# First keys read in halves, the first maxima's rows sent ahead, and unused products in TensorE's wait

## The reference

```python
q, k, v = split(x @ W_qkv.T + b_qkv)                   # 32 x 256 tokens, 16 heads of 8
p = softmax(einsum('bthd,bshd->bhts', q, k) / sqrt(8))
x = layernorm(x + (p @ v) @ W_out.T + b_out)
scores = sigmoid(x @ gate_w.T)                          # 8 experts, the best two of scores + bias
y = shared(x) + sum of two experts(x * score) * score   # each silu(x w1) * (x w3) @ w2
x = layernorm(x + y)
```

## Time and profile before

| | |
|---|---|
| median of the runs | 765.87 us (764.38 to 766.14) |
| the profiled execution | 764.94 us |
| its span, first to last instruction | 763.1 us |
| TensorE busy | 740.5 us, 97% |
| VectorE busy | 630.9 us, 83% |
| ScalarE busy | 521.4 us, 68% |
| GpSimd busy | 500.8 us, 66% |
| mean granted TensorE clock | 0.98 of full speed |

### The profile page before, as it was taken

The page is one execution under the profiler, slowest core; times in us unless marked ns, Lnnn a source line. Parts: engine busy times, 40 slices in busy tenths (PEclk is TensorE's granted clock), DMA queues, the critical chain, the costliest instruction groups (busy, mean ns, idle before and its releaser), DMA issues.

```text
span 763.1 us, 20494 instructions
## 1 busy us (share of the span) xinstructions
PE 740.5 (97%) x7004; PEld 531.6 (70%) x7004; DVE 630.9 (83%) x1353; ACT 521.4 (68%) x1069; POOL 500.8 (66%) x714
## 2 busy tenths in 40 slices
PE   4899999999999999999999999999999999999996
PEld 2456665665666566566554788888888888888886
DVE  6889999999999999999997657988666766666676
ACT  3289899998988889898888646454454544455442
POOL 7356888878777787877624755566565655655564
PEclk8599999999999999999999999999999999999999
DMA  6667666675665556656611745454554544455440
GB/s 171 179 160 190 182 174 185 169 191 162 168 172 156 172 148 169 171 160 174 154 32 43 203 116 115 118 130 117 152 128 128 126 127 129 129 125 124 125 106 29
DMA packets 202369, 108.93 MB, mean 143 GB/s; under 512 B 10537, under 2 KB 202281, under 8 KB 202281
## 3 DMA queue, kind: packets, MB, share of 16 engines
q1 hardware_dynamic: 198560, 105.22, 52.9%
q10 hardware_dynamic: 3720, 2.57, 1.4%
HBM read 73.41 MB, written 33.82 MB: 141 GB/s over the span
## 4 chain that ended last, share of the span: by engine, by line
PE 93%; DVE 2%; DMA 1%; issue 1%; ACT 1%; POOL 1%; ACTq 0%; POOLq 0%; SPq 0%; DVEq 0%
PE bank L1037 17%; PE bank L841 16%; PE bank L810 11%; PE bank L848 9%; PE bank L849 9%; PE bank L850 9%; PE bank L826 8%; PE bank L934 3%; PE bank L904 3%; PE bank L958 2%; PE bank L965 1%; PE bank L990 1%; DVE negmax L1188 1%; PE bank L869 1%; PE bank L974 1%
## 5 line engine op out<-in xcount | busy, mean ns | idle before, releaser
L1188 DVE TENSOR_REDUCE negmax<-bank 128x2 f32<-128x512 f32 x512 | 322.9, 679 | 16.1 <-PE bank L826 13.7
L666 ACT ACTIVATE probs<-bank 128x512 f32<-128x512 f32 x512 | 294.2, 613 | 47.7 <-PE bank L810 43.8
L784 ACT ACTIVATE q_stack<-k_stack 128x512 f32<-128x512 f32 x128 | 80.8, 631 | 152.3 <-DVE k_stack L1247 152.1
L826 PE MATMUL bank<-k_stack,q_stack 48*128 48x256 bf16 x1024 | 163.5, 281 | 8.8 <-DMA q_stack<-q_parts_dram 6.1
L810 PE MATMUL bank<-q_stack,k_stack 50*128 50x256 bf16 x1024 | 157.7, 274 | 0.7 <-ACT probs L666 0.4
L1247 DVE TENSOR_TENSOR k_stack<-bank,probs 128x512 f32<-128x512 f32 x128 | 88.3, 689 | 71.0 <-PE bank L850 69.5
L841 PE MATMUL bank<-probs,v_aug 128*32 128x256 f32 x2048 | 137.6, 386 | 0.2 <-ACT attT L677 0.2
L848 PE MATMUL bank<-x_hi,hi_w 128*128 128x512 f32 x288 | 126.5, 439 | 1.3 <-DVE res L1200 0.5
L810 PEld LDWEIGHTS bank<-q_stack,k_stack 50*128 50x128 bf16 x1024 | 75.9, 95 | 72.2 <-issue 35.3
L849 PE MATMUL bank<-x_hi,lo_w 128*128 128x512 f32 x288 | 114.2, 396 | 0.0
L850 PE MATMUL bank<-x_lo,hi_w 128*128 128x512 f32 x288 | 113.7, 395 | 0.0
(11 more groups left out here) (132 smaller groups left out, 1198.2 us busy)
## 6 DMA issues: line engine op xcount, KB each, us to landing
probs<-route_dram SPq DMA_DIRECT2D x128, 256.0 KB, 5.0
k_stack<-k_parts_dram SPq DMA_DIRECT2D x64, 192.0 KB, 4.1
q_stack<-q_parts_dram SPq DMA_DIRECT2D x62, 192.0 KB, 3.4
q_parts_dram<-q_parts SPq DMA_DIRECT2D x32, 192.0 KB, 2.1
k_parts_dram<-k_parts SPq DMA_DIRECT2D x32, 192.0 KB, 2.2
k_parts_dram<-k_parts SPq DMA_DIRECT2D x32, 128.0 KB, 2.0
q_parts_dram<-q_parts SPq DMA_DIRECT2D x32, 128.0 KB, 2.1
x_sb<-x SPq DMA_DIRECT2D x32, 128.0 KB, 2.2
```

The lines of the kernel that those rows point to most:

```text
L666: nc.scalar.activation(probs[h][:], score_ps[bank(b, h)][:].rearrange("p (j t) -> p j t", j=NT), ACT.Exp).then_inc(exp_done, 1)
L784: nc.scalar.activation(act[n % DEPTH], gated[n % DEPTH] if n else up1_ps[0][:], ACT.Silu).then_inc(act_set, 1)
L826: mm = pe.matmul(max_ps[bank(b, h)][:, i * T:(i + 1) * T], q_stack[b.ring][first:last, h // 2, i * P:(i + 1) * P], k_stack[b.ring][first:l ...
L1188: nc.vector.tensor_reduce(negmax[b.ring % 2][:, :, column], max_ps[bank(b, head)][:].rearrange("p (i s) -> p i s", i=NT), AX_X, ALU.max, n ...
```

## The change

The first batch's keys are read with four DMAs in two halves with a semaphore each. Batch 0's rows of maxima are sent at the head of SyncE's slot -1, and only the first of their two DMAs is SyncE's; the second is ScalarE's, at the end of its slot -1. For batch 0 the transposes move from p = 4 to p = 5, and VectorE's copy from step 9 to step 11. TensorE gets products of a constant tile that nobody reads: four in slot -4, sixteen in slot -2 at p = 3, and one at the head of each pair of slots -2 and -1 in which row maxima are found (four and eight). The constants of the fourth ring are GpSimd's now.

```diff
+            def row_maxima_in(b):                                    # SyncE
+                sp.wait_ge(max_rows_set, b.count(1, 1))
+                for u in range(2 if b.c else 1):
+                    sp.dma_start(q_stack[b.ring][HALF * u + ROWS:HALF * u + ROWS + 2, :, :],
+                                 max_rows[H * u:H * u + H, :]).then_inc(max_in[b.ring], 16)
             def first_stack(b):
                 sp.wait_ge(first_k_out, 16 * PARTS)
-                for u in range(2):
-                    sp.dma_start(k_stack[b.ring][HALF * u:HALF * u + ROWS, :, :],
-                                 k_parts_dram[b.ring].rearrange("(g u) d c t -> u (d c) g t", u=2)[u]).then_inc(first_k_in, 16)
+                for n in range(2):
+                    pairs = slice(n * PAIRS // 2, (n + 1) * PAIRS // 2)
+                    for u in range(2):
+                        sp.dma_start(k_stack[b.ring][HALF * u:HALF * u + ROWS, pairs, :],
+                                     k_parts_dram[b.ring].rearrange("(g u) d c t -> u (d c) g t", u=2)[u][:, pairs, :]).then_inc(first_k_in[n], 16)
             def slot(t):
+                if t.neg.c == 0:
+                    row_maxima_in(t.neg)
                 b = t.stack
...
-                    sp.wait_ge(k_ones, b.c + 1)
+                    if b.c < RING - 1:
+                        sp.wait_ge(k_ones, b.c + 1)
+                    else:
+                        sp.wait_ge(fourth_set, 1)
...
-                b = t.neg
-                if b.live:
-                    sp.wait_ge(max_rows_set, b.count(1, 1))
-                    for u in range(2):
-                        sp.dma_start(q_stack[b.ring][HALF * u + ROWS:HALF * u + ROWS + 2, :, :],
-                                     max_rows[H * u:H * u + H, :]).then_inc(max_in[b.ring], 16)
+                if t.neg.live and t.neg.c:
+                    row_maxima_in(t.neg)
...
+            r = RING - 1                                             # GpSimd
+            pool.memset(k_stack[r][:].rearrange("p h t -> p (h t)").bitcast(F32), TWO_ONES).then_inc(fourth_set, 1)
+            pool.memset(v_aug[r][:], 0.0).then_inc(fourth_set, 1)
+            pool.wait_ge(fourth_set, 2)
+            for u in range(2):
+                ins = pool.memset(v_aug[r][:, :, u, :, 2 * D + u:2 * D + u + 1], 1.0)
+            ins.then_inc(fourth_set, 1)
...
                 if t.proj.live and h == ACT_LOAD:                    # ScalarE, end of its slot
...
+                if t.neg.c == 0:
+                    act_e.wait_ge(max_rows_set, 1)
+                    act_e.dma_start(q_stack[0][HALF + ROWS:HALF + ROWS + 2, :, :], max_rows[H:2 * H, :]).then_inc(max_in[0], 16)
...
-                    pe.wait_ge(first_k_in, 32)                       # TensorE
+                    pe.wait_ge(first_k_in[h // (H // 2)], 32)
...
+            def fill(ps, count):
+                for _ in range(count):
+                    pe.matmul(ps[:], filler[:, 0:P], filler[:], start=True, stop=True)
             def slot(t, first=0, last=PAIRS):
                 for p in range(first, last):
+                    if (t.soft.c, p) == (-4, 0):
+                        pe.wait_ge(filler_set, 1)
+                        fill(max_ps[0], 4)
+                    if (t.soft.c, p) == (-2, PE_VQ + 1):
+                        fill(max_ps[0], 16)
+                        pe.wait_ge(qk_f, 3)
+                    if t.soft.c in (-2, -1) and t.maxima(2 * p)[0].live:
+                        fill(score_ps[0], 1)
...
-                    if b.live and p == PE_TOK:
+                    if b.live and p == (PE_TOK if b.c else PE_TOK + 1):
...
+            dve.memset(filler[:].bitcast(F32), TWO_ONES).then_inc(filler_set, 1)   # VectorE, first
             clear_keys(0)
             clear_keys(1)
             clear_values(0)
...
             clear_values(1)
-            for r in (2, 3):
-                clear_keys(r)
-                clear_values(r)
-            dve.wait_ge(v_clear, 2 * RING)
+            clear_keys(2)
+            clear_values(2)
+            dve.wait_ge(v_clear, 2 * (RING - 1))
...
-                        if t.neg.live:
+                        if t.neg.live and t.neg.c:
                             dve.wait_ge(max_T, t.neg.count(1, 1))
...
-                    if b.live and h == DVE_TOK:
+                    if b.live and h == (DVE_TOK if b.c else DVE_TOK + 2):
+                        if b.c == 0:
+                            dve.wait_ge(max_T, 1)
```

More of the change, by code:

```diff
@@ L116, in attention_moe_layer @@
         attT = sb("attT", [P, 2, T])
+        filler = sb("filler", [P, 512], BF16)
         recip_sum = sb("recip_sum", [P, 8 * NT, 2])
@@ L133, in attention_moe_layer @@
         max_rows_ps = misc[0:2 * H, 3 * P:4 * P].bitcast(BF16)
+        filler_set = sem("filler_set")
         wv_in, bv_in = sem("wv_in"), sem("bv_in")
@@ L140, in attention_moe_layer @@
         wqk_hi_set, wqk_lo_set, xT_hi_set, xT_lo_set = (sem(n) for n in ("wqk_hi_set", "wqk_lo_set", "xT_hi_set", "xT_lo_set"))
+        fourth_set = sem("fourth_set")
         k_ones, v_clear, consts_set = sem("k_ones"), sem("v_clear"), sem("consts_set")
@@ L146, in attention_moe_layer @@
         stack_in = [sem(f"stack_in{r}") for r in range(RING)]
-        first_k_out, first_q_out, first_k_in = sem("first_k_out"), sem("first_q_out"), sem("first_k_in")
+        first_k_out, first_q_out = sem("first_k_out"), sem("first_q_out")
+        first_k_in = [sem(f"first_k_in{n}") for n in range(2)]
         first_q_in = [sem(f"first_q_in{n}") for n in range(2)]
@@ L702, in slot @@
                             act_e.wait_ge(av_mm, b.count(4, 4 * (1 - RING)))
+                        elif b.c < RING - 1:
+                            act_e.wait_ge(v_clear, 2 * (b.c + 1))
                         else:
-                            act_e.wait_ge(v_clear, 2 * (b.c + 1))
+                            act_e.wait_ge(fourth_set, 3)
                         for u in range(2):
```

## The result

The changed kernel takes 770.20 us (median, 768.28 to 770.98) against 765.87: ratio 1.0058, 95% interval 1.0046 to 1.0069. It is 4.3 us slower, outside the range I gave (763.0 to 769.6), and on the side of my slower rival. Its profiled execution has a span of 768.5 us against 763.1, 5.4 us more.

A forecast was written before the change was run, and what follows sets the result against it. TensorE has no pause from about 32 us, so only slot 1's start counts: slot 0 2.3 us later, less 0.6 of half clock, is +1.7 on 764.94, 766.6; the median shown is 0.9 above, 767.6, range 763.0 to 769.6.

The forecast's parts named there:

- my slower rival: Thin work from 15 to 29 us doesn't hold the clock; slot 0 at 37.9, total 771.0; chance 0.14.
- The chain copy, first row DMA, load, ScalarE, second row DMA: Before slot 0: ScalarE's row DMA waits for batch 4's load behind SyncE's; slot 0 starts at 34.6, 2.3 us later.
- clock 1.00 at 13 to 29: A sign to look for: TensorE at full clock from the first wait through the row maxima.
- the clock holds here: In the wait for the queries, sixteen unread products leave 2.4 us idle, under the 3.8 after which the clock fell.
- are hidden: In the row maxima, twelve singles of 0.22 us each at 2.4 GHz fit inside a pair's 1.21 us of reductions.
- At full clock the first reduction starts: Batch 0's maxima: first reduction 0.43 us behind the first product instead of 0.69, at 15.5.
- VectorE's two gaps: In batch 0's maxima, the gaps of 0.59 and 1.45 us shrink to some 0.2 together (0 to 0.8).
- my third rival: The half-clock case in the maxima: slot 0 at 37.9, +5.1 us, total 771.0; chance 0.14.
- The second row DMA: ScalarE's row DMA before slot 0, issued at 31.6 beside batch 2's stack reads, lands in 3.0 us.
- Slot 0: First part at 1.2 GHz, 6.5 us of half clock (5 to 8) against 8.0 before: 0.6 less.
- Clock held to slot 0's end: Rival: clock holds through the wait at 29 to 34.6, slot 0 takes some 10.3; total 765.1; chance 0.32.
- Rows as early as before: Rival: batch 0's rows aren't held by the load, slot 0 starts at 30.6 at full clock; total 761.1; chance 0.12.

The follow-up runs named there:

- e1: The changed kernel with SyncE issuing batch 4's load of x transposed ahead of its wait for the copied maxima; 765.26 us, ratio 0.9999.
- e6: The changed kernel with batch 4's load ahead of the wait for the copied maxima and without the twelve single unread products; 764.15 us, ratio 0.9987.
- e7: The changed kernel with batch 4's load ahead of the wait for the copied maxima, without the sixteen and the twelve unread products; 764.39 us, ratio 0.9989.
- e12: The changed kernel without the twelve single unread products, nothing else; 768.63 us, ratio 1.0048.
- e9: The changed kernel with batch 3's and 4's loads early, three unread products for each single and nine more at slot 0's head; 763.65 us, ratio 0.9983.
- e11: The kernel of e9 with the copy and its transposes back at step 9 and p = 4; 761.70 us, ratio 0.9956.
- e2: The changed kernel with both row DMAs on SyncE, at the same place; 766.44 us, ratio 1.0015.
- e4: The kernel before with all the unread products (4, 16, 12) and nothing else; 765.85 us, ratio 1.0010.
- e5: The changed kernel with batch 4's load ahead of the wait for the copied maxima and batch 3's load at the start; 764.90 us, ratio 0.9995.
- e8: Keys halved, row DMAs split but SyncE's behind stack reads, batch 3's load at start, copy at step 9, only the first four unread products; 764.87 us, 0.9994.
- e3: The kernel before with the keys read in halves and nothing else; 765.12 us, ratio 0.9997.

## Why the prediction was wrong

**Right in mechanism.** The chain copy, first row DMA, load, ScalarE, second row DMA is there link by link: load issued 0.96 us behind the copy (0.8 forecast), landing 2.14 (2.5), ScalarE's issue at once. e1 shows it carries the whole loss. The clock was down when slot 0 began. GpSimd's memsets took 0.95 us each, as worked out, and hid. TensorE's sixteen products took 3.5 us in the wait.

**The step that failed** is "clock 1.00 at 13 to 29". The prediction's "the clock holds here" came true for the wait up to 13.87; the same paragraph and the next carry it on through the row maxima (the singles "are hidden", "At full clock the first reduction starts"), and there it failed. I had asked only how long TensorE stands idle, since the one fall in the trace came in an idle stretch, and took it that any work holds the clock. It fell at 19.1 in the maxima. VectorE's two gaps were then 1.45 and 1.81 us, 3.26 together, for the 0.2 forecast: **3.1 us**. Of these 1.8 are half clock without the singles (2.04 in e6, e7 and e12; at 2.4 GHz in e9 and e11, with three products a pair, the same two gaps are 0.29 and 0.74), 0.9 the singles (2.90 in e1) and 0.4 the wait for batch 3's load, which the prediction put at nothing. With the first product 1.2 earlier than forecast, the copy was 1.8 late (30.03 for 28.2). The trace of before had a hint, as my third rival says itself: the same work had not raised the clock in 17 us. I gave it 0.14 because raising and holding seemed two things, and they are: with the singles in it this work let the clock fall in every run but raised it again in some (changed at 25.9, e2 at 26.6, e4 at 27.3), not in e1 and e5. That rival's 771.0, slot 0 at 37.9, is the nearest of my four to what came, 37.25 and 770.2. Part of that is luck: its copy was 1.6 us too late and its slot 0 0.9 too short.

**Sizes off in the rest of the sum.** The second row DMA landed in 4.05 us where I took 3.0, 1.05 more and within my bounds of 2.0 to 4.5. The rule of the Trainium skill that I cited (page "DMA: Bandwidth & Descriptors", section "Queues, rings and completion order": engines take turns between queues) would have made it 2.0. Measured beside reads are 4.05, 3.98, 4.12 and 3.56 us (changed, e12, e8, e11), and 2.4 ahead of them, so here the trace doesn't agree with what I drew from the rule. Nor was the 2.0 us of the earlier trace rows a DMA "alone", as I wrote: batch 2's last stack read, issued at 26.99, landed at 30.95, in the middle of it. What the traces show is that the row DMA lands just behind a stack read issued at nearly the same time (the numbers are at the end). Nor does the trace agree with it for the keys: by turns their cut should not touch the queries, and it gave them 1.5 us (4.49 to 3.01); I had seen only that their own issue doesn't change, and not that half of the keys' bytes would now go behind them. Slot 0 took 13.8 us, with 9.2 at half clock where I took 6.5, for 12.85: 1.0. Two slips in the sums change nothing in the forecast: 15.95 + 16 x 0.607 + 0.59 + 1.45 is 27.7, and 28.2 + 0.6 + 0.3 is 29.1.

Together: first product -1.2, gaps +3.1, landing and its neighbours +0.8, slot 0 +1.0: 3.7 on top of the 1.7 forecast is the 5.4 of the spans.

**The rivals.** Clock held to slot 0's end: not in this kernel; with three products for one and nine more it held (e11), and slot 0 was then 10.56 us, 10.3 in the rival. Rows as early as before: excluded by the earlier trace rows and what the trace after shows.

## What to carry to other kernels

When a DMA is moved to another engine's queue "in parallel", list what that engine waits for ahead of it, and who issues that; here one load behind a wait on one engine held the other for 7 us and cost the whole change 4.9. A filler for TensorE's clock has to be measured in the clock's row over the whole stretch that it is to cover: too little of it cost 1 us and bought a clock that fell anyway; three times as much, with nine products more, held it in e11 and won 0.44%, and lost it in about half of e9's executions, where the nine then stood in slot 0's way. And an earlier start is worth only what it saves at the clock that it runs at.

## What the runs showed of the hardware that I had not expected

- TensorE's clock fell from 2.4 to 1.2 GHz with the engine 0.81 busy in the microsecond before (e4 at 17.0), and in the changed kernel at 19.1 behind 5 us of row maxima with one unread product a pair and pauses of at most 0.2 us. With three a pair it stayed at 2.4 GHz there in both runs that had them (e9 until 27.4, behind a wait of 1.87 us; e11 throughout, with a wait of 1.19).
- The sixteen products that fill the first wait don't lengthen it: first product at 13.74 without (e7) and 13.89 with them (e6).
- Reading each 192 KB of keys as two halves of 96, so that the second halves are issued behind the other queue's first two 96 KB reads, brought the first product forward in every run that has it (13.55 to 14.04, against 15.26 and 15.44 without). I have no run that says by what mechanism.
- A row DMA of 8 KB lands in 2.4 us ahead of the stack reads and in 3.0 to 4.1 where reads issued ahead of it are in flight, on the reads' queue (e3, e8) or on the other. In four runs it lands 0.04 to 0.23 us behind the last 192 KB read issued ahead of it: read 37.17 and row 37.21 (changed), 35.73 and 35.96 (e12), 32.90 and 33.08 (e8), 32.10 and 32.24 (e3). In e11 that read lands at 32.02, the next one, issued 0.14 us behind the row DMA, at 32.81, and the row at 32.88. In the kernel before, issued 3.3 us behind the last read, the row DMA took 1.9.
